# A fused adaLN block, minimal GRU, coupled recurrence and routed FFN on one core: the hand-over to the recurrence's loop is rearranged

## What is computed

```python
x = x + _L0_attn_ref(_L0_cond_ref(x, cond, ...), Wz, bz, Wn, bn)      # adaLN attention + MLP, then minimal GRU over time
x = x + _L0_ffn_ref(_L0_cond2_ref(cond, cond, x, coupling, bias), Wr, br, W1, W2)
# minimal GRU: per feature over 32 times, h' = (1 - z) h + z g
#   z = sigmoid(x Wz + bz);  n = x Wn + bn;  g = n + 0.5 if n >= 0 else sigmoid(n)
# recurrence (_L0_cond2_ref): 32 Runge-Kutta steps, 4 stages each
def _derivative(q, p, drive, coupling, bias):
    i_couple = jnp.tanh(q) @ coupling.T
    dq = q - q ** 3 / 3.0 - p + drive + i_couple + bias
    dp = EPSILON * (q + ALPHA - BETA * p)
    return (dq, dp)
# _L0_ffn_ref: 16 blocks of a GELU MLP, the top 4 of a router kept
```

## Time and profile before

| what | value |
|---|---|
| median of 3 runs | 477.7 us (477.31 to 478.11) |
| the profiled execution, its own time | 477.12 us |
| its span, first to last instruction | 475.3 us |
| PE, DVE, ACT, POOL busy | 459.7, 388.6, 316.7, 47.6 us |
| the hand-over from late output to loop | about 283 to 298 us of the span |
| the loop's 32 steps | from about 297.5 us to the end |

### The profile page before, as it was taken

How to read it: one execution, slowest core, us unless ns; L and a number is a source line. 1 busy time by engine, 2 the same in 40 slices (tenths; PEclk the granted TensorE clock), 3 DMA queues, 4 the chain that set the end, 5 groups by cost and what they waited for, 6 DMA issues and landing times.

```text
span 475.3 us, 13759 instructions
## 1 busy us (share of the span) xinstructions
PE 459.7 (97%) x5268; PEld 333.2 (70%) x5268; DVE 388.6 (82%) x1392; ACT 316.7 (67%) x951; POOL 47.6 (10%) x77
## 2 busy tenths in 40 slices
PE   6999999999999999999999999999999999999997
PEld 4455776457755776558735456789898988989886
DVE  3979885869758899998799889788888788888874
ACT  1678873788567874887668684756665756656563
POOL 3011240222220240223000000000000000000000
PEclk9999999999999999999999999999999999999999
DMA  8992501110202000000000000000000000000000
GB/s 273 422 401 76 124 21 59 29 59 23 67 1 66 22 0 2 0 2 1 1 0 2 0 1 0 3 3 3 3 11 1 11 1 11 1 11 12 0 12 23
DMA packets 10404, 20.91 MB, mean 44 GB/s; under 512 B 1473, under 2 KB 4993, under 8 KB 9729
## 3 DMA queue, kind: packets, MB, share of 16 engines
q1 hardware_dynamic: 9808, 19.89, 12.4%
q10 hardware_dynamic: 560, 0.60, 0.4%
HBM read 19.40 MB, written 1.08 MB: 43 GB/s over the span
## 4 chain that ended last, share of the span: by engine, by line
PE 82%; DVE 8%; ACT 5%; issue 2%; DMA 2%; POOL 1%; SPq 0%; DVEq 0%; ACTq 0%
PE bank L983 54%; PE score L983 26%; DMA ao_sb<-xtok 2%; PE spare L983 1%; POOL ptx L517 1%; ACT th L862 1%; ACT ptx L641 1%; ACT ao_sb L594 1%; DVE drive_pair L2163 1%; DVE drive L1590 1%; ACT x L541 0%; DVE drive L1594 0%; DVE q_group L2380 0%; ACT pscaled L871 0%; DVE ao_sb L2029 0%
## 5 line engine op out<-in xcount | busy, mean ns | idle before, releaser
L983 PE MATMUL bank<-x,pairs_store 128*128 128x512 f16 x384 | 86.3, 379 | 0.5 <-ACT x L541 0.4
L983 PEld LDWEIGHTS bank<-x,pairs_store 128*128 128x128 f16 x384 | 36.9, 98 | 43.4 <-issue 1.4
L517 POOL TENSOR_TENSOR ptx<-pt,ptx 32x256 f16<-32x256 f32 x62 | 43.2, 698 | 176.7 <-ACT ptx L641 173.2
L983 PE MATMUL score<-cub,neg_eye 128*128 128x64 f32 x256 | 55.5, 298 | 0.0
L594 ACT ACTIVATE big<-bank,head_b 128x512 f16<-128x512 f32 x60 | 39.8, 685 | 17.4 <-PE bank L983 17.0
L2253 DVE TENSOR_TENSOR thlo<-th 128x64 f16<-128x64 f32 x128 | 28.8, 225 | 26.3 <-ACT th L863 25.0
L983 PE MATMUL score<-th,coup_part 128*128 128x32 f16 x1024 | 46.3, 177 | 2.0 <-ACT th L862 0.7
L983 PE MATMUL bank<-pairs_store,ao_sb 128*128 128x256 f16 x360 | 43.0, 273 | 0.7 <-issue 0.2
L983 PE MATMUL bank<-pairs_store,x 128*128 128x512 f16 x192 | 43.4, 379 | 0.0
L862 ACT ACTIVATE th<-score 128x64 f16<-128x64 f32 x96 | 21.4, 223 | 32.2 <-PE score L983 29.6
L983 PEld LDWEIGHTS score<-th,coup_part 128*128 128x128 f16 x1024 | 34.6, 96 | 6.7 <-ACT th L862 4.5
(11 more groups left out here) (279 smaller groups left out, 1048.8 us busy)
## 6 DMA issues: line engine op xcount, KB each, us to landing
wqk_sb<-wqk SPq DMA_DIRECT2D x16, 256.0 KB, 2.8
wv_sb<-wv SPq DMA_DIRECT2D x4, 512.0 KB, 5.8
wo_sb<-wo SPq DMA_DIRECT2D x4, 512.0 KB, 4.2
f_sb<-ffn_w SPq DMA_DIRECT2D x2, 1024.0 KB, 14.5
ao_sb<-xtok SPq DMA_DIRECT2D x4, 256.0 KB, 6.3
x_sb<-xT SPq DMA_DIRECT2D x1, 1024.0 KB, 12.4
w_sb<-w1T SPq DMA_DIRECT2D x1, 1024.0 KB, 15.4
w_sb<-w2T SPq DMA_DIRECT2D x1, 1024.0 KB, 16.2
```

Source lines behind the costliest of these rows:

```text
L517: nc.gpsimd.tensor_tensor(ptx[s, 1, :, s], pt[s], ptx[s, 0, :, s], ALU.subtract).then_inc(ptx_ready, 1)
L983: return nc.tensor.matmul(dst, lhsT, rhs, start=start, stop=stop, **kw)
```

## The change

Three things are rearranged, with no arithmetic added or left out.

1. The linear forms quarter and keep of the early times are made by ScalarE (`early_gates`), two activations for each block, instead of by VectorE (two `tensor_scalar` for each block). The counts of `early_gate` go from 3 to 5 for each block, and VectorE's waits follow.
2. On ScalarE the loop's first tanh pair and the four scaled copies of p stand ahead of `late_tangent(0)` and `late_relu(0)`.
3. In `first_round` of ScalarE nothing stands any more in stages 0, 4, 8 and 12. Late z of the second block goes from n = 4 to 7, its quarter from 7 to 9, its keep from 8 to 10, the second `drive_bias` from 12 to 13. On VectorE one of the two scans at the end of step 3 goes to the next stage, the two behind it move down one place, and the last of them lands in stage 5 of the second group, between two operations of the router's top-4.

```diff
--- before.py
+++ after.py
@@ -812,9 +812,13 @@
             def early_gates(ob):
 
                 src = score[:, 1 - ob]
+                z, cand, pos, quarter, keep = (early_store[:, ob, w] for w in range(5))
                 act.wait_ge(early_full, ob + 1)
-                gate_z(ob, src[:, NE:2 * NE], early_store[:, ob, 0], early_gate)
-                gate_n(ob, src[:, 0:NE], early_store[:, ob, 1], early_store[:, ob, 2], early_gate, early_gate)
+                gate_z(ob, src[:, NE:2 * NE], z, early_gate)
+                gate_n(ob, src[:, 0:NE], cand, pos, early_gate, early_gate)
+                act.wait_ge(early_gate, 5 * ob + 1)
+                nc.scalar.activation(quarter, z, ACT.Identity, bias=one_quarter, scale=0.25).then_inc(early_gate, 1)
+                nc.scalar.activation(keep, z, ACT.Identity, bias=one_half, scale=-0.5).then_inc(early_gate, 1)
 
             def late_part(ob, w):
                 return late_store[:, ob, w, :, 1:SPAN]
@@ -856,7 +860,6 @@
             early_gates(1)
             drive_bias(2, 3, EARLY)
             drive_bias(3, 4, EARLY)
-            late_tangent(0)
             def tanh_of(src, unit):
 
                 nc.scalar.activation(th16[:].rearrange("p (k b) -> p k b", k=KB), src, ACT.Tanh, scale=unit).then_inc(th16_ready, 1)
@@ -888,27 +891,25 @@
 
             def first_round(n):
 
-                if n == 0:
-                    late_relu(0)
-                elif n == 1:
+                if n == 1:
                     late_z(0)
                 elif n == 2:
                     late_quarter(0)
                 elif n == 3:
                     late_keep(0)
-                elif n == 4:
-                    late_z(1)
                 elif n == 5:
                     late_tangent(1)
                 elif n == 6:
                     late_relu(1)
                 elif n == 7:
+                    late_z(1)
+                elif n == 9:
                     late_quarter(1)
-                elif n == 8:
+                elif n == 10:
                     late_keep(1)
                 elif n == 11:
                     drive_bias(2, 5, LATE, front)
-                elif n == 12:
+                elif n == 13:
                     drive_bias(2, 6, LATE, back)
 
             def group_round(i, n):
@@ -947,9 +948,12 @@
                 for j in range(4):
                     scale_p(j)
 
+            scale_all(0, 0)
+            late_tangent(0)
+            late_relu(0)
             for i in range(2):
                 for n in range(4 * UNROLL):
-                    if n % 4 == 0:
+                    if n % 4 == 0 and i + n > 0:
                         scale_all(i, n // 4)
                     if i == 0:
                         first_round(n)
@@ -1377,7 +1381,7 @@
             pe.wait_ge(x3_ready, 2 * KB + 1)
             late_gate(LATE_N[0], wn_sb, 0, 0)
             late_gate(LATE_Z[0], wz_sb, 0, 0)
-            pe.wait_ge(early_gate, 3 * KB)
+            pe.wait_ge(early_gate, 5 * (KB - 1) + 3)
             unread(score[:, 0], 1)
             mm(score[:, 1], scaled_eye[:], ptx[:, 0, 0:G // 2].rearrange("p g n -> p (g n)"), True, True).then_inc(seeded, 1)
             pe.wait_ge(x3_ready, 3 * KB)
@@ -2086,15 +2090,14 @@
 
             def early_gru(ob):
 
-                z, cand, pos, quarter, keep, state = (early_store[:, ob, w] for w in range(6))
-                dve.wait_ge(early_gate, 3 * ob + 1)
-                own.step(V.tensor_scalar(quarter, z, 1.0, 0.25, ALU.add, ALU.mult))
-                own.step(V.tensor_scalar(keep, z, -0.5, 0.5, ALU.mult, ALU.add))
-                dve.wait_ge(early_gate, 3 * ob + 3)
+                cand, pos, quarter, keep, state = (early_store[:, ob, w] for w in range(1, 6))
+                dve.wait_ge(early_gate, 5 * ob + 3)
                 own.step(V.scalar_tensor_tensor(pos, cand, 0.0, pos, ALU.min, ALU.add))
                 own.wait()
+                dve.wait_ge(early_gate, 5 * ob + 4)
                 own.step(V.scalar_tensor_tensor(cand, pos, 1.0, quarter, ALU.add, ALU.mult))
                 own.wait()
+                dve.wait_ge(early_gate, 5 * ob + 5)
                 keep0, cand0 = (ap.rearrange("p (b t) -> p b t", b=NBH)[:, :, 0:1] for ap in (keep, cand))
                 own.step(V.scalar_tensor_tensor(cand0, keep0, 0.5, cand0, ALU.mult, ALU.add))
                 own.wait()
@@ -2333,12 +2336,12 @@
                     late_low(0, 0)
                 elif at == 15:
                     done["scan", 1, 0] = late_scan(1, 0, done["term", 1, 0])
-                    done["scan", 1, 1] = late_scan(1, 1, done["term", 1, 0])
 
             def second_round(at):
 
-                if at in (0, 1):
-                    done["scan", 1, 2 + at] = late_scan(1, 2 + at, done["term", 1, 1])
+                if at in (0, 1, 5):
+                    part = (0, 1, 5).index(at) + 1
+                    done["scan", 1, part] = late_scan(1, part, done["term", 1, part // 2])
                 elif at in (6, 7):
                     late_drive(1, at - 6, done["scan", 1, 2 * (at - 6) + 1])
                 elif at == 8:
```

## The result

The changed kernel has a median of 474.38 us over 6 runs (474.12 to 474.87), the kernel before 477.54 us over 6 runs (477.08 to 478.11); the ratio is 0.9941 with a 95% interval of 0.9928 to 0.9955. That is 3.16 us less. The forecast was 475.7 us, 1.95 us less, in a range of 474.9 to 477.0 us. The profiled execution takes 474.39 us, with a span of 472.6 us.

What follows compares the result with a forecast made beforehand. VectorE was taken to bound up to 296 us, then one chain through ScalarE, VectorE and TensorE. Gains 0.96 + 0.84 + 0.25 - 0.10 = 1.95 us off 477.7 gave 475.7 us, range 474.9 to 477.0 us.

Steps and rivals of the forecast that it cites:

- Part 1: Hand-over near 295 us: linear forms leave VectorE's gapless run, TensorE's last late gates start 0.4 to 0.54 us earlier, taken 0.5.
- The two-semaphore waits: Two VectorE instructions wait on two semaphores: 0 to 0.03 us for each of four, 0.05 us in all.
- Part 2: Loop start: first coupling follows the drive matmuls sooner, 0.29 us; stage 1's tanh no longer held, 0.17 us more.
- Part 3: Steps 1 to 3: emptied first stages gain 0.84 us, one scan moved out 0.25 us, its return costs 0.1 us.
- Emptied first stages: First stages of steps 1, 2, 3 without late ScalarE operations: gains 0.25 + 0.30 + 0.32, less 0.01 each, 0.84 us.
- the scan's move: End of step 3 on VectorE: one of two scans ahead of the write to `score` moved out, gain 0.25 us.
- the scan's return: Stage 5 of the second group: the moved scan delays the coupling, minus 0.1 us, bounds 0 and 0.27.
- The front carries: Rival denied it: TensorE's matmuls at 295.06 us or double waits take most of 0.5 us; gain 1.25 us, chance 0.14.
- Moved work does not pay again: Rival claimed moved operations cost 0.84 us again and the scan all its 0.27 us; gain 0.94 us, chance 0.08.
- The change is on the path: Rival denied it: TensorE's fillers pace each stage, ScalarE's and VectorE's gains become waiting; 477.7 us, chance 0.02.
- The loop's rhythm is the same: Rival claimed later steps fall into a slower rhythm, at 0.1 us a step 478.6 us; chance 0.04.
- The likeliest case: The forecast itself, hand-over through step 5: gains of 1.6 to 2.3 us, chance 0.72.

Runs made afterwards that it cites:

- part 1 alone: Kernel before with only quarter and keep of the early times moved to ScalarE: 476.00 us, ratio 0.9990.
- part 2 alone: Kernel before with only the first tanh pair and scaled copies put ahead of the late tangent and relu: 476.12 us, ratio 0.9989.
- part 3 alone: Kernel before with only late operations moved out of first stages of steps 1, 2, 3 and one scan moved: 475.45 us, ratio 0.9972.
- the scan: Whole change, but VectorE keeps its two scans at the end of step 3 and none in stage 5 of the second group: 474.69 us.
- late z put back: Whole change, but the second block's late z returns from n = 7 to n = 4: 474.67 us.

## Why the prediction was wrong

**The step that failed is the base from which its sum subtracts the gain.** The prediction took its gain off "the median of 477.7" of three runs, with 0.4 us as the spread of single runs. On three chips the kernel before has 70 runs since: 48 at full clock with means of 476.44 to 476.84 us, and 22 with a fall of the clock, 0.8 to 1.3 us above those in the mean. Against such a base the forecast of 1.95 us would have read 474.5 to 474.9 us, and the changed kernel measures 474.36 to 474.56 us at full clock. A better gain would not have saved the forecast: 477.7 us less the measured 2.1 us is 475.6 us.

Why the base was so high stays open. All six runs of the kernel before in the first comparison took 477.08 us or more; of the 70 later ones 26 did. If the six had been drawn from the same mixture, that would happen some 3 times in 1000 (an estimate, 26/70 to the sixth power), so falls at their usual rate are a poor explanation. Only the profiled execution's clock is known there, 1.0, and it reached its first square root 0.36 to 0.66 us later than the other profiles here, as shown above. A chip that slows every program is not the reason either, as the changed kernel's six runs beside it read 474.38 us, as they do elsewhere.

**The falls may also be a small part of the gain.** Kernels without the moves of part 3 had 30 falls in 93 runs (kernel before 22 of 70, part 1 alone 5 of 11, part 2 alone 3 of 12), kernels with them 3 in 53 (the changed kernel 3 in 17, the others none in 36). At 0.95 us a fall this is worth (0.32 - 0.06) x 0.95 = 0.25 us in the mean. The count leans the same way on each chip (without the moves 15 of 48, 2 of 11 and 13 of 34; with them 2 of 13, none of 24 and 1 of 10), but the kernels with the moves include variants, and the one without the unread matmuls is left out. That part 3 does it is a count, not an experiment, and by what, nothing here shows. The prediction did not have this term.

**Part 1, right, 0.09 us too small by the times, 0.16 us by the trace.** The gates could start at 295.06 + 0.43 us, TensorE's distance between starts, and not at the end of the matmul in front that was taken as a bound; and the first of them costs 0.69 us instead of 0.75 us when it follows without a wait. Alone it gives 0.59 us in the times, 0.66 us in the trace. The two-semaphore waits cost nothing that shows: the three operations from the first on start 0.33 and 0.32 us apart, and 0.32 and 0.33 us before. ScalarE's form takes 0.29 us between starts, where the estimate was 0.27 us.

**Part 2, right.** Expected 0.46 us; alone it gives 0.48 us in the trace, 0.40 us in the times. One slip stands in its working: 298.37 + 1.47 is 299.84 us and not 299.88 us, which would have made the sum 0.04 us larger.

**Part 3, right in its mechanism.** Emptied first stages 0.80 us (0.84 forecast); the scan's move 0.25 us, as forecast; the scan's return 0.00 us, not 0.10 us. The prediction saw that the remainder's matmuls wait for the second tanh anyway and still charged 0.10 of the 0.14 us; the whole of it is hidden.

**The sum.** Traces give 1.09 + 0.80 + 0.25 + 0.01 = 2.15 us, times 2.10 and 2.12 us at full clock, against 1.95 us forecast: 8% too small. The stretch up to step 1 took 17.95 us in the trace used here and 17.93 to 18.04 us in eight others of kernels with parts 1 and 2, so the traces fix the 1.09 us no better than 1.00 to 1.11 us. The lower end of the range should have been 475.4 - 0.4 = 475.0 us by the prediction's own rule, not 474.9 us; the measured time lies below either.

**The rivals.** The front carries (part 1 alone). Moved work does not pay again (part 3 alone, the scan). The change is on the path (late z put back). The loop's rhythm is the same: from step 7 on 5.12 to 5.16 us a step in both kernels. The likeliest case was right in its mechanism and its gain; the range around it was built on a wrong centre and knew nothing of the clock, because the one trace at hand had it at full level throughout.

## What to carry to other kernels

Before a forecast is hung on a median of a few runs, ask whether the runs form one group; here the profiled execution, at full clock, lay 0.6 us below the median, and was itself 0.3 to 0.7 us above the full-clock means measured later. An instruction's price is that of its place: the same activation costs 0.23 us between a step's scaled copies and its next tanh, and nothing three stages on; a copy of 0.54 us costs 0.16 us ahead of the write that TensorE waits for and 0.06 us behind it (step 7 with the copy in its second stage, against 5.14 us without). And a linear operation may go to the engine that is dearer for it, if that engine is idle where it stands.

## What the runs showed of the hardware

- TensorE's granted clock can fall to 1.2 GHz (0.50) in the midst of the recurrence's loop and be back at 2.4 GHz 3.4 us later; worked out from the clocks of the stretches, all four profiled falls last that long. Ahead of it TensorE was busy for 3.66 of 4 us and then 0.87 of 1 us (kernel before), for 1.49 of 2 us (whole change) and for 4.93 of 5 us (no unread matmuls). The same 2 us of the whole change's first profile, 306 to 308 us, show 1.57 us busy and no fall. Of 70 runs of the kernel before 22 had one; the three falls profiled in the first group all lie in step 2. A fall costs 0.8 to 1.3 us (difference of the means of hit runs and full-clock runs of one kernel on one chip).
- The 12 small matmuls of each later group that nobody reads keep the clock up: without them 11 of 12 runs have one fall or more, with times up to 5 us longer; with them no profile here shows a fall in the loop past step 2. In the one run without a fall their absence gained nothing (474.51 against 474.56 us), so they cost next to nothing.
